# A four-block attention model on one core: batches in straight line, dense by both experts, an output projection begun ahead, and another order of the first loads

## What is computed

```python
# L0: cross attention with 16 heads of 64 over 1601 context rows, then a feed-forward net
q = layernorm(x) @ Wq * scale;  k, v = split(media @ Wkv)
attn = softmax(where(mask, q @ k.T, -inf));  out = (attn @ v).reshape(..., 1024)
x = x + tanh(attn_gate) * (out @ Wo)
x = x + tanh(ff_gate) * (gelu(layernorm(x) @ W1) @ W2)
# L1 and L3: memory attention of one head over the context, a gate, an rms norm
m = memory @ W_mem.T;  ctx = softmax(x @ m.T / sqrt(D)) @ m
x = rmsnorm(x + sigmoid(concat(x, ctx) @ W_gate.T + b) * ctx)
# L2: causal self attention (16 heads of 16), cross attention (16 heads of 8), SwiGLU
vm = (types[:, :-1] == 1) & (types[:, 1:] == 1)      # an expert for each token
mixed = where(vm, h @ v_qkv, h @ l_qkv);  ctx = sdpa(rope(q), rope(k), v, causal)
x = x + where(vm, ctx @ v_dense, ctx @ l_dense)
x = x + sdpa(h @ cq, enc @ ck, enc @ cv) @ cdense
x = x + where(vm, v_mlp(h), l_mlp(h))
```

## Time and profile before

| | us |
|---|---|
| median of 3 runs | 2342.53 (2340.41 to 2343.27) |
| profiled execution, its own time | 2338.46 |
| its span | 2336.5 |
| PE busy | 2001.2 (86%) |
| PE weight loads busy | 1480.0 (63%) |
| DVE busy | 1299.6 (56%) |
| ACT busy | 922.0 (39%) |
| POOL busy | 766.5 (33%) |
| instruction loads, 16 KB each (queue q8) | 105 |

### The profile page before, as it was taken

How to read it: one execution, slowest core, us unless ns; L and a number is a source line. 1 busy time by engine, 2 the same in 40 slices (tenths; PEclk the granted TensorE clock), 3 DMA queues, 4 the chain that set the end, 5 groups by cost and what they waited for, 6 DMA issues and landing times.

```text
span 2336.5 us, 34832 instructions
## 1 busy us (share of the span) xinstructions
PE 2001.2 (86%) x11932; PEld 1480.0 (63%) x11932; DVE 1299.6 (56%) x2036; ACT 922.0 (39%) x1718; POOL 766.5 (33%) x676
## 2 busy tenths in 40 slices
PE   3999787898799978799889988879888997886986
PEld 2776576556676657655677756755577775774655
DVE  6666245655666523575566652467457663346733
ACT  1555132470355413256045541326515552231731
POOL 3788310001287821000237870100025876110000
PEclk8999898799899989879899998988989998897998
DMA  4000200201000010100100001020000001102000
GB/s 174 13 8 7 108 1 1 82 2 48 27 10 12 37 75 1 50 33 6 43 27 13 8 37 75 1 81 1 22 29 26 10 8 65 46 1 81 1 1 5
DMA packets 17612, 74.58 MB, mean 32 GB/s; under 512 B 2320, under 2 KB 9744, under 8 KB 13968
## 3 DMA queue, kind: packets, MB, share of 16 engines
q1 hardware_dynamic: 16848, 69.55, 8.1%
q10 hardware_dynamic: 576, 2.62, 0.3%
HBM read 71.12 MB, written 1.05 MB: 31 GB/s over the span
## 4 chain that ended last, share of the span: by engine, by line
PE 69%; DVE 16%; issue 7%; ACT 5%; POOL 1%; DMA 0%; SPq 0%; DVEq 0%; ACTq 0%; POOLq 0%
PE x L860 28%; PE pv L860 18%; PE st L860 16%; PE mi L860 6%; DVE k_hi_lo L1473 2%; ACT k_hi_lo L633 2%; DVE prob_sums L1848 1%; DVE max_cross L1873 1%; DVE max_parts L1547 1%; DVE q_lo_shift L1556 1%; PE x L981 1%; ACT ck_stack L763 1%; DVE x_normed L1639 1%; DVE recip_sum L1755 1%; DVE recip_sum L1664 1%
## 5 line engine op out<-in xcount | busy, mean ns | idle before, releaser
L566 POOL TENSOR_TENSOR prob_sums<-prob_sums,probs 128x512 f32<-128x512 f32 x352 | 455.4, 1294 | 49.7 <-ACT probs L675 13.8
L675 ACT ACTIVATE probs<-st 128x512 f32<-128x512 f32 x416 | 228.2, 596 | 310.6 <-PE st L860 294.1
L1547 DVE TENSOR_REDUCE max_parts<-x 128x1 f32<-128x832 f32 x256 | 251.0, 1020 | 126.3 <-PE x L860 124.5
L549 POOL TENSOR_TENSOR rstd_work<-rstd_work 128x2 f32<-128x2 f32 x24 | 16.6, 693 | 829.4 <-DVE rstd_work L1470 829.4
L1873 DVE TENSOR_REDUCE max_cross<-x 128x1 f32<-128x512 f32 x384 | 238.5, 684 | 71.7 <-PE x L860 69.2
L860 PE MATMUL st<-q_hi_hi,k_hi_lo 128*128 128x256 f32 x832 | 231.4, 309 | 28.9 <-DVE q_lo_shift L1556 15.6
L860 PE MATMUL pv<-probs,v 128*64 128x256 f32 x1664 | 231.0, 396 | 3.7 <-DVE recip_sum L1664 3.7
L860 PEld LDWEIGHTS st<-q_hi_hi,k_hi_lo 128*128 128x128 f32 x832 | 159.6, 192 | 106.9 <-issue 97.7
L860 PE MATMUL st<-q_lo_shift,k_hi_rows 128*128 128x256 f32 x832 | 210.6, 285 | 0.0
L860 PE MATMUL x<-ck_stack,cq_blocks 128*128 128x512 f32 (+1 forms) x512 | 195.4, 454 | 0.9
L860 PEld LDWEIGHTS st<-q_lo_shift,k_hi_rows 128*128 128x128 f32 x832 | 160.5, 193 | 0.0
(11 more groups left out here) (289 smaller groups left out, 4143.1 us busy)
## 6 DMA issues: line engine op xcount, KB each, us to landing
w_gate_up<-in_wgu SPq DMA_DIRECT2D x4, 3072.0 KB, 10.0
w_ff<-in_w SPq DMA_DIRECT2D x8, 1024.0 KB, 5.9
w_qk<-in_wqk SPq DMA_DIRECT2D x4, 2048.0 KB, 8.3
w_pair<-in_w SPq DMA_DIRECT2D x32, 192.0 KB, 2.3
w_down<-in_wdn SPq DMA_DIRECT2D x4, 1536.0 KB, 13.3
w_dense<-in_wd SPq DMA_DIRECT2D x4, 1024.0 KB, 11.0
mask_ints<-in_mask SPq DMA_DIRECT2D x4, 832.0 KB, 4.3
ctx_t_raw<-in_ctxT SPq DMA_DIRECT2D x4, 832.0 KB, 6.1
```

The costliest lines, as they stand in the source:

```text
L566: pool.tensor_tensor(acc[:, 0], acc[:, 0], prob[:, kt % 4], ALU.add).then_inc(add_pool.handle, 1)
L675: act.activation(prob[:, kt % 4], ST[kt % 2][:], ACT.Exp, scale=HD0 ** -0.5).then_inc(p_exp.handle, 1)
L1547: dve.tensor_reduce(mxs[:, qt, h, half:half + 1], X[n % 2][:].rearrange("p (c n) -> p c n", c=2)[:, :, 0:QUART], AX.XY, ALU.max).then_inc( ...
```

## The change

**Batches in straight line.** `for b in range(B): body(b, b < B - 1)` on all engines. No branch, no register arithmetic, and every `sem_inc(passed)` is gone, so that the wait is carried by the instruction behind it.

The core of the diff:

```diff
@@ gpsimd, prologue
                 pool.wait_ge(batch_ready.handle, batch_ready.at(b))
-                pool.sem_inc(passed.handle, 1)
                 if first:
+                    pool.wait_ge(const_t.handle, const_t.at(0))
+                    pool.wait_ge(x0t_read.handle, x0t_read.at(0))
                     fill_keys(0)
                     fill_keys(1)
@@ every engine
-            with pe.Fori(0, B - 1) as b:
-                body(b, True)
-            body(B - 1, False)
+            for b in range(B):
+                body(b, b < B - 1)
@@ tensor
-                pe.wait_ge(norm.handle, norm.at(b * PAIRS + PAIRS - 1))
-                for t in range(TT):
-                    for p in range(PAIRS):
-                        m = mm(X[0][:, t * D:(t + 1) * D], attn[:, p, t * P:(t + 1) * P], wo[:, p], p == 0, p == PAIRS - 1)
+                pe.wait_ge(norm.handle, norm.at(b * PAIRS + PAIRS - 2))
+                for last in range(2):
+                    if last:
+                        pe.wait_ge(norm.handle, norm.at(b * PAIRS + PAIRS - 1))
+                    for t in range(TT):
+                        for p in ((PAIRS - 1,) if last else range(PAIRS - 1)):
+                            m = mm(X[0][:, t * 512:t * 512 + D], attn[:, p, t * P:(t + 1) * P], wo[:, p], p == 0, p == PAIRS - 1)
@@ tensor, dense
-                mm(X[0][:, 0:512], cc[:, C_SELS], cx[:, 2:4].rearrange("p k n -> p (k n)")).then_inc(cn_sum.handle, 1)
-                pe.wait_ge(cxm_ready.handle, cxm_ready.at(b))
+                pe.wait_ge(cxm_ready.handle, cxm_ready.at(b, 1))
+                mm(MI[:, 0:512], cc[:, C_SELS], cx[:, 2:4].rearrange("p k n -> p (k n)")).then_inc(cn_sum.handle, 1)
+                for half in range(2):
+                    pe.wait_ge(cxm_ready.handle, cxm_ready.at(b, half + 1))
+                    for t in range(TT):
+                        for e2 in range(2):
+                            for k in range(2 * half, 2 * half + 2):
+                                m = mm(X[e2][:, t * 512:t * 512 + D], cx[:, k, t * P:(t + 1) * P], wd[:, e2, k], k == 0, k == 3)
@@ vector, memory_layer
-                    ts(qs[:], r32(cth[:, 0:NT]), 0.0, ck[:, K_SHQ:K_SHQ + 1])
@@ vector, x0_normed
                 ts(rs[:, 0], mv[:, :, 1], EPS[0], None, ALU.add, ALU.bypass).then_inc(var0_ready.handle, 1)
+                if b == 0:
+                    const_cast()
                 dve.wait_ge(rstd0_ready.handle, rstd0_ready.at(b))
```

More of the change, by code:

```diff
@@ L184, in program @@
         rs = sb("rstd_work", [P, 5, TT])
+        tokens = sb("token_types", [P, 2, TT], I32)
+        expert = sb("token_expert", [P, 2, TT])
         mxs = sb("max_parts", [P, 2, 4, 2])
@@ L188, in program @@
         rec = sb("recip_sum", [P, NT])
+        qs = sb("q_shift", [P, NT], F32R)
         acc = sb("prob_sums", [P, 2, 512])
@@ L237, in program @@
         q1h, q1l = place("q1_hi", [P, NT], F32R, f), place("q1_lo", [P, NT], F32R, f)
-        qs = place("q_shift", [P, NT], F32R, f)
+        f[0] += 1024
         pct = place("pc_t", [P, NT], F32, f)
@@ L433, in load_next, with first @@
                     sp.wait_ge(wv_split.handle, wv_split.at(b * DUOS + d - 1))
-                    sp.sem_inc(passed.handle, 1)
                     load_duo(d)
+            def first(dst, src):
+                sp.dma_start(dst, src).then_inc(first_in.handle, 16)
             load_early(0)
+            first(cc[:], io["const_f"][:, 0:N_CR])
+            first(ck[:], io["const_k"])
+            first(feat[:], io["feat"])
+            load_pair(0)
             load_ctx(0)
-            load_pair(0)
             load_duo(0)
+            const(craw_const[:], io["const_r"])
+            const(ctrig[:], io["const_f"][:, N_CR:N_C])
+            const(wck[:], io["wckv"])
+            const(gates[:], io["gates"].partition_broadcast(P))
+            const(rows[:], io["rows"].partition_broadcast(P))
+            const(posi[:], io["pos"].partition_broadcast(P))
+            assert n[0] == CONSTS * 16
             load_rows(0)
@@ L610, in body @@
                 rsqrt(6)
-            with pool.Fori(0, B - 1) as b:
-                body(b, True)
-            body(B - 1, False)
+            for b in range(B):
+                body(b, b < B - 1)
         @block.scalar
@@ L653, in first_values @@
                 values(b, 0, c, ST[c % 2])
+            act.wait_ge(const_in.handle, CONSTS * 16)
+            act.activation(tgate[:], gates[:], ACT.Tanh).then_inc(const_r.handle, 1)
             context(0)
             queries(0, 0)
+            act.wait_ge(const_t.handle, const_t.at(0))
             keys(0, 0, 0)
@@ L850, in body @@
                 memory_layer(1)
-            with act.Fori(0, B - 1) as b:
-                body(b, True)
-            body(B - 1, False)
+            for b in range(B):
+                body(b, b < B - 1)
         @block.tensor
@@ L862, in _ @@
             ident, ones = cc[:, C_ID], cc[:, C_ONES]
-            pe.wait_ge(const_in.handle, CONSTS * 16)
-            pe.wait_ge(const_t.handle, const_t.at(0, 1))
-            for k, tab in enumerate((C_COS, C_SIN)):
-                for ch in range(2):
-                    last = mm(MI[:, k * NT:(k + 1) * NT], ctrig[:, tab - N_CR + ch], onehot[:, ch], ch == 0, ch == 1)
-            last.then_inc(const_r.handle, 1)
+            pe.wait_ge(first_in.handle, first_in.at(0))
             def x0_transposed(b):
@@ L960, in _ @@
             x0_transposed(0)
+            pe.wait_ge(const_in.handle, CONSTS * 16)
+            pe.wait_ge(const_t.handle, const_t.at(0, 2))
+            for k, tab in enumerate((C_COS, C_SIN)):
+                for ch in range(2):
+                    last = mm(X[1][:, k * NT:(k + 1) * NT], ctrig[:, tab - N_CR + ch], onehot[:, ch], ch == 0, ch == 1)
+            last.then_inc(const_r.handle, 1)
+            for n in range(4):
+                mm(PV[:], ident, cc[:].rearrange("p k n -> p (k n)"))
             prep_q(0, 0, 0)
+            pe.wait_ge(const_t.handle, const_t.at(0))
             prep_k(0, 0, 0, 0)
@@ L1606, in context @@
                 tt(ctl[:, c], craw[:, c], r32(cth[:, c]), ALU.subtract).then_inc(ctl_ready.handle, 1)
+            dve.wait_ge(first_in.handle, first_in.at(0))
+            clink(dve.memset(rs[:, 1], -0.5))
             mask_sum(0)
@@ L1917, in body @@
                 assert count[0] == chain.per, count[0]
-            with dve.Fori(0, B - 1) as b:
-                body(b, True)
-            body(B - 1, False)
+            for b in range(B):
+                body(b, b < B - 1)
 _CONST = ("const_r", "const_f", "const_k")
```

113 lines of the change are left out of this document (42 added, 71 removed).

## The result

| | before | changed |
|---|---|---|
| median, us | 2342.9 (2340.41 to 2343.7) | 2306.26 (2304.52 to 2306.86) |
| profiled execution, us | 2338.46 | 2304.52 |
| its span, us | 2336.5 | 2302.7 |
| mean granted clock of TensorE | 0.911 | 0.921 |

The account below looks back on a forecast made before the run. The prediction took PE to bound the kernel, with gains only at the seams. Terms -11.2 - 4.6 - 1.3 - 11.2 - 24 + 2 = -50.3 us, from 2342.5 to 2292; range 2279 to 2305, 8 in 10.

Parts of the forecast that it names:

- the change takes nothing from the pairs: Within the pairs PE is the limit; the change takes nothing there but small waits, and gains lie at the seams.
- the dense layer: Self attention's dense product: 7.0 us sooner per batch, DVE's added instructions +1.0, net 6.0; x4 = 24 us (15 to 25).
- The signs that were to show the parts at work: Profile after: gaps before first scores at most 1.3 us, POOL's fills from 33 to 37, first maxima 47 to 54, x_a some 7 sooner.
- signs of being wrong: Batches 0 to 2 differing from batch 3, `const_in` landing below 21 or above 29 us, or half clock inside the pairs.
- The loop: Ends of batches: each of two taken turns costs PE 5.5 us plus 0.2 for the longer branch; -11.2 us.
- rivals 3 and 4: First: the turn's cost moves, 2296 or 2303, chance 0.07. Second: slower through instruction loads in straight line, 2355, chance 0.02.
- The carriers: Norms: dropping instructions that carry waits saves 0.12 us before `bn_aggr` and 0.10 before POOL; 21 x 0.22 = 4.6 us.
- I take 0: The other carriers of waits, on POOL where PE does not wait: 0, with up to 3 us for the range.
- q_shift: Second memory layer: DVE's copy of the transposes waits for q_shift's slow filling; 3 batches x 0.45 = 1.3 us won.
- The projection: w_o after the pairs: 28 rows start directly, 8 at half clock and 24 at full; 2.8 us x4 = 11.2 (6 to 12.4).
- The start: Before the first scores: constants land at 25.5 us, first maxima at 49.5 instead of 47.8; taken as +2 us (-0.8 to +6.4).

Follow-up runs that it names:

- loop_only: The kernel before with only the batches written out in straight line, the instructions that carry waits kept: 2326.4 us, ratio 0.9935.
- q_shift_again: The changed kernel with q_shift filled again at the start of each memory layer, as before the change: 2314.6 us, ratio to the kernel before 0.9887.
- projection_only: The kernel before with seven pairs of the output projection ahead of the last, and nothing else: 2331.6 us, ratio 0.9956.
- dense_only: The kernel before with self attention's dense by both experts and the small load of token types, loop and other loads as before: 2331.3 us, ratio 0.9961.
- loop_and_carriers: The kernel before with batches written out and without the instructions that carry waits (`passed` dropped): 2333.4 us, ratio 0.9961.
- more_unneeded: The changed kernel with 20 instead of 12 unneeded products ahead of the transposes for cross attention: 2295.5 us, ratio to the kernel before 0.9790.
- memset_later: The changed kernel, but POOL clears v_cross only after the transposes of the feed-forward net's norm: 2284.8 us, ratio to the kernel before 0.9763.

## Why the prediction missed

Two steps failed: that the change takes nothing from the pairs, and what the dense layer gives. The signs that were to show the parts at work came as named: 1.0 us ahead of the first scores, POOL's fills from 36.1, first maxima at 53.1, x_a 7.0 us sooner behind the second reciprocal. Two of the signs of being wrong came too: stages of batches 0 to 2 that differ from those of batch 3, and a clock at half inside a pair.

**The loop: right.** -11.2 forecast, -10.1 in the stages, -11.5 by loop_only's span. The gap of 6.5 us is 1.0 at both turns, and straight line has no price that the runs show (96 instruction loads of 16 KB instead of 105): rivals 3 and 4 are out.

**The carriers: the step that failed.** The small waits went as said: 0.03 instead of 0.15 ahead of bn_aggr, and POOL 0.08 us after DVE (0.15 in about half of the norms, so 3 to 4 us rather than 4.6). But "the change takes nothing from the pairs but small waits" and "I take 0" for POOL's other carriers were wrong. In straight line the carriers keep POOL's rows off DVE's split, as in batch 3 of before and in loop_only; at the ends of batches 0 and 1 before, the split lay within PE's gap at the branch, with POOL idle. With both gone the first pairs of batches 1 to 3 take 9.3 us more. The rows were there to be read: x_normed at 3.54 us beside POOL's memset, 0.6 in the other norms, q_shift at 1.37 and 0.34. I knew the pattern at that norm and did not look for it where the change moves POOL against DVE.

**q_shift: mechanism right, size wrong.** -1.3 forecast, -8.3 in the stage, and 8.3 by q_shift_again. The term counted the wait of 0.45 us and not the clock behind it.

**The projection: right.** -11.2 forecast, -11.7 in the stages, -10.3 by projection_only. The 32 rows of batch 2 take 8.56 us, the first 3.4 us at half clock and the rest at full, which is the 8 and 24 rows of the forecast.

**The dense layer: the second step that failed.** To the end of the products the stages give -24.8 us: in each batch the 7.0 of the forecast, less 2.9 in batch 3, where more of the stage ahead of the second reciprocal now runs at half clock. Behind it the forecast had only DVE's 1.0 per batch. The added steps cost 1.1 (1.82 us from x_a's start to bn_stats instead of 0.73), and the clock some 2 us more in three batches. The term is -15.0, not -24, and -9 (6 to 12) in dense_only. The prediction asked when the clock rises ahead of the end, and not when it falls behind it. (Its bounds of 4.5 and 6.0 us per batch make 18 to 24; the stated 15 to 25 is wider than they are.)

**The MLP: +2.1, not 0.** Its clock is 0.90 instead of 0.93 in three batches. dense_only shows that (+3.2), but so does loop_and_carriers (+2.6), which has the dense layer of before. Which part of the change brings it is open.

**The start: +5.1, not +2.** Constants at 26.2 instead of 25.5; POOL's fills 8.94 us instead of 6.8, since now they lie beside DVE's splits (the same lock); the query fills 4.9 instead of 4.5. So the first maxima come at 53.1 instead of 49.5.

Together, measured against forecast: loop -10.1 and -11.2, pairs +7.4 and 0, projection -11.7 and -11.2, carriers -3.3 (taken as the stage from w_o to w_qk) and -4.6, dense -15.0 and -24, MLP +2.1 and 0, q_shift -8.3 and -1.3, start +5.1 and +2: -33.8 and -50.3. That q_shift gave 7 us more than forecast is luck: without it the two sums would lie 23.5 us apart instead of 16.5. The range failed with the sum, because its upper end counted the clock as a gain that stays away, never as one that is given back, and had nothing for the pairs. The parts run alone (-9, -9, -10, q_shift's -8, and +5 for the start) add to -31 against -36.6; with intervals of 3 to 5 us each that is no sign of anything else.

## What to carry to other kernels

An instruction that does nothing may keep two engines apart: when a wait or a carrier is taken from POOL, look at which of DVE's steps from SBUF to SBUF then start beside a row of POOL, and price those as ending with POOL's row. When a gap of PE is closed, follow the granted clock past the end of the stage: here an idle of 2.3 us behind it took 2 of 7 us back. A stage may also gain or lose 3 us of clock by an edit that lies elsewhere, so read an edit's price from several batches and runs. And idle time ahead of a norm's transposes is worth filling (10.8 us in more_unneeded), or better, its cause is made short (21.5 us in memset_later).
